# Gated delta layer, products P and A: two heads alternate on two row groups, exponentials ahead of the third copy, two unread products fewer

## The reference, cut to what matters

```python
def _step(S, xs):
    qt, kt, vt, gt, bt = xs
    S = S * jnp.exp(gt)[..., None, None]
    pred = jnp.einsum('bhk,bhkv->bhv', kt, S)
    delta = (vt - pred) * bt[..., None]
    S = S + jnp.einsum('bhk,bhv->bhkv', kt, delta)
    return (S, jnp.einsum('bhk,bhkv->bhv', qt, S))
```

## Time and profile before

| what | us |
|---|---|
| median of 3 runs | 1492.69 (1489.96 to 1498.32) |
| the profiled execution, its own time | 1490.81 |
| its span | 1489.1 |
| granted clock of TensorE, mean over the span | 0.939 of full |
| PE, DVE, ACT, POOL busy | 1355.1, 895.7, 695.8, 277.0 |
| the block of the change, from the first transposition to the end of the last L1509 | 396.6 to 429.3 |

### The profile page before, as it was taken

The page is one execution under the profiler, slowest core; times in us unless marked ns, Lnnn a source line. Parts: engine busy times, 40 slices in busy tenths (PEclk is TensorE's granted clock), DMA queues, the critical chain, the costliest instruction groups (busy, mean ns, idle before and its releaser), DMA issues. The chain is left out here.

```text
span 1489.1 us, 32883 instructions
## 1 busy us (share of the span) xinstructions
PE 1355.1 (91%) x13699; PEld 748.7 (50%) x13707; DVE 895.7 (60%) x2139; ACT 695.8 (47%) x1038; POOL 277.0 (19%) x343
## 2 busy tenths in 40 slices
PE   7999997998578987989999989988699999989989
PEld 3355554464346773644555454445245555564436
DVE  3899984646685456649999555323455555525331
ACT  5578786635373226536777732102344444442110
POOL 4331431002320000043000001101433433200210
PEclk9999998999788998999999989999599999989999
DMA  3323301000300000032221030002100000000000
GB/s 88 65 35 69 67 3 33 1 2 0 114 1 4 16 1 15 1 61 34 37 43 24 3 103 0 0 9 48 20 12 16 15 13 15 7 1 1 1 0 28
DMA packets 33958, 37.48 MB, mean 25 GB/s; under 512 B 9153, under 2 KB 24626, under 8 KB 33810
## 3 DMA queue, kind: packets, MB, share of 16 engines
q1 hardware_dynamic: 33810, 35.39, 10.9%
HBM read 18.43 MB, written 1.07 MB: 13 GB/s over the span
## 5 line engine op out<-in xcount | busy, mean ns | idle before, releaser
L586 DVE TENSOR_REDUCE row_max_pieces<-psum 128x1 f32<-128x512 f32 (+3 forms) x672 | 407.1, 647 | 123.1 <-PE psum L481 121.0
L685 ACT ACTIVATE probs<-psum 128x1024 f32<-128x1024 f32 (+7 forms) x384 | 343.5, 899 | 218.2 <-PE psum L481 217.8
L535 PE MATMUL psum<-probs,v_ones 128*32 128x256 f32 (+1 forms) x2688 | 239.2, 377 | 8.5 <-POOL probs L470 4.1
L481 PE MATMUL psum<-q_all,k_head 97*32 97x512 f32 (+3 forms) x1536 | 192.3, 492 | 3.5 <-issue 3.5
L481 PE MATMUL psum<-k_stack,q_stack 96*32 96x512 bf16 x2048 | 162.6, 387 | 5.4 <-DVE row_max_pieces L586 3.1
L481 PE MATMUL psum<-q_stack,k_stack 97*32 97x512 bf16 x2048 | 160.7, 385 | 0.0
L535 PEld LDWEIGHTS psum<-probs,v_ones 128*32 128x32 f32 x2688 | 88.2, 109 | 85.5 <-POOL probs L470 21.1
L481 PE MATMUL psum<-k_head_bf,q_all_bf 80*32 80x512 bf16 (+3 forms) x768 | 96.2, 347 | 5.0 <-POOL q_all_bf L2500 3.6
L481 PEld LDWEIGHTS psum<-q_all,k_head 97*32 97x32 f32 x1536 | 78.8, 110 | 34.4 <-issue 8.6
L481 PEld LDWEIGHTS psum<-k_stack,q_stack 96*32 96x32 bf16 x2048 | 57.9, 97 | 72.2 <-DVE row_max_pieces L586 20.4
L481 PEld LDWEIGHTS psum<-q_stack,k_stack 97*32 97x32 bf16 x2048 | 59.1, 97 | 51.1 <-ACT probs L685 3.7
(11 more groups left out here) (363 smaller groups left out, 2085.3 us busy)
## 6 DMA issues: line engine op xcount, KB each, us to landing
q_stack<-arena SPq DMA_DIRECT2D x32, 96.0 KB, 2.6
k_stack<-arena SPq DMA_DIRECT2D x32, 96.0 KB, 2.6
arena<-gd_g_sums SPq DMA_DIRECT2D x6, 512.0 KB, 6.1
q_stack<-arena SPq DMA_DIRECT2D x32, 64.0 KB, 2.3
k_stack<-arena SPq DMA_DIRECT2D x32, 64.0 KB, 2.3
x_tokens<-in_x SPq DMA_DIRECT2D x4, 256.0 KB, 3.2
k_stack<-arena SPq DMA_DIRECT2D x32, 32.0 KB, 2.3
q_stack<-arena SPq DMA_DIRECT2D x32, 32.0 KB, 2.0
```

Of the source, the lines that this page charges most:

```text
L481: last = pe.matmul(o[j:j + 32], by[:, j:j + 32], rows, **flags)
L535: last = pe.matmul(psum[32 * g:32 * g + VW, PVB, a - g * D:D], V[:, c, h, :], pr[:, n % PB, a:(g + 1) * D], start=(c == 0), stop=(c == (2 ...
L586: last = dve.reduce_max(mx[:, h % 2, qt, i:i + 1], o[:, 0:plain], AX.X)
L685: act.activation(pr[:, n % PB, q_from(c):], psum[:, 2 * (n % 2):2 * (n % 2) + 2, :].rearrange("p a n -> p (a n)")[:, q_from(c):], ACT.Exp, ...
```

## The change

- `p_and_a(n)` now does pieces n and n+1 together, for even n: for each j it multiplies the chunk of head h, then that of head h+1, on the neighbouring 32 rows and into the other slot.
- The wait for `a_done` stands once for the pair and is for n-1: pieces up to n-2 have been read.
- The turns stand after j = 0 and j = 1 (in the first pair after j = 0, 1 and 2), two for a pair.
- `keep_busy` is gone from the head of pieces 0, 2 and 4; one stands behind the first pair. With the one ahead of the third `turn`, two remain of four.
- ACT: `decays(0)` stands ahead of keep(2).

```diff
-                TURNS_IN = ((3, 4), (5,)) + tuple((m,) for m in range(6, len(turns)))
+                TURNS_IN = ((3, 4, 5),) + tuple((m, m + 1) for m in range(6, len(turns), 2))
...
-                            h, half = blocks[n]
-                            f, rows = h // 4, slice(32 * (h % 4), 32 * (h % 4) + 32)
+                            (h, half), f = blocks[n], blocks[n][0] // 4
                             for odd in range(2):
                                 pe.wait_ge(kept[odd], (EACH * (2 * f + half + 1) + 1 - odd) // 2)
-                            if n >= 3:
-                                pe.wait_ge(a_done, n - 2)
-                            if n in (0, 2, 4):
-                                keep_busy(pe, 2 + 2 * (n % 3), 1)
+                            if n >= 2:
+                                pe.wait_ge(a_done, n - 1)
                             for j in range(4):
                                 cols = slice((4 * half + j) * P, (4 * half + j + 1) * P)
-                                last = pe.matmul(slot(n)[:, j // 2, j % 2], KNT[rows, f, cols], QKT[rows, :, f, cols],
-                                                 start=True, stop=True)
-                                if j == 3:
-                                    last.then_inc(pa_in, 1)
-                                if j % 2 and j // 2 < len(TURNS_IN[n]):
-                                    turn(TURNS_IN[n][j // 2])
+                                for i in range(2):
+                                    rows = slice(32 * ((h + i) % 4), 32 * ((h + i) % 4) + 32)
+                                    last = pe.matmul(slot(n + i)[:, j // 2, j % 2], KNT[rows, f, cols], QKT[rows, :, f, cols],
+                                                     start=True, stop=True)
+                                    if j == 3:
+                                        last.then_inc(pa_in, 1)
+                                if j < len(TURNS_IN[n // 2]):
+                                    turn(TURNS_IN[n // 2][j])
...
-                        for n in range(len(blocks)):
+                        for n in range(0, len(blocks), 2):
                             p_and_a(n)
+                            if n == 0:
+                                keep_busy(pe, 6, 1)
...
                         keep(0)
+                        decays(0)
                         keep(2)
-                        decays(0)
                         decays(1)
```

## The result

| | before | after |
|---|---|---|
| median of the runs (4 each), us | 1492.87 (1489.96 to 1498.32) | 1508.51 (1507.98 to 1515.4) |
| ratio | | 1.012, 95% interval 1.0099 to 1.014 |
| span of the profiled execution, us | 1489.1 | 1506.2 |
| mean granted clock | 0.939 | 0.930 |

A forecast was written before the change was run, and what follows sets the result against it. PE, which does not rest, was taken to bound the block, with DVE last at its end. Waits less savings 4.3 plus clock fall 10.4 gave 14.7 us: 1505.5 on the profiled execution, 1507.4 on the median; said 1506, range 1494 to 1513.

The forecast's parts named there:

- The head: Block start through first pair: first product 0.95 us earlier, second pair at 406.3 against piece 2 at 407.74, gaining 1.4 us.
- The price of 0.20 + 0.43k: PE's time in us for k products on each of two row groups side by side: 0.63, 1.06, 1.49.
- The wait: Ahead of later pairs PE waits 1.64 us for DVE's reading; pairs 5.08 against 3.26 us, block +4.3 at held clock.
- The rival of the wait that does not bite: PE runs ahead into the next pair, its queue stays full; block ends 3.0 us earlier, 1487.8; chance 0.06.
- the rival of serial products: Alternating products do not overlap, 1.72 us more per pair; +14.6, again about 1506; chance 0.07.
- The clock: In the changed block the granted clock falls near 412 to 414 and does not come back: +10.4 us.
- three and a half pairs: Number of pairs taken to run at half clock, 2.96 us more each: +10.4; bounds one and a half and five.
- The pair at half clock: Products, turns and wait of one pair after the clock falls: 8.04 us, 2.96 more than at full clock.
- The rival of the held clock: The clock holds and the wait stays: +4.3 us, 1495.1 to 1497.0; chance 0.27.
- the two unread products: Products nobody reads, dropped from PE's work in the block: 1.06 us saved each, included in the +4.3.
- the x8 row: PE timeline row before the change: four products of two adjoining pieces take what two take alone, so overlap already exists.

The follow-up runs named there:

- e_last: Changed kernel with the two turns of each pair, from the second pair on, moved behind the pair's last products, into the wait: 1494.34 us, ratio 1.0009.
- e_busy: Changed kernel with one unread product of 512 columns in each of the four waits ahead of pairs 4, 6, 8 and 10: 1496.11 us, ratio 1.0038.
- e_fewer: Kernel before the change, without the unread products at the heads of pieces 2 and 4: 1501.67 us, ratio 1.0061.
- e_mix: Changed kernel's head, then from piece 2 on the order and waits of before, without further unread products: 1502.89 us, ratio 1.0057, runs in two groups.
- e_wait: Kernel before the change, with the pair's stricter wait (a_done for n-1) at even pieces and the old product order: 1497.72 us, ratio 1.004.

## Why the prediction was right

*The head.* Forecast: first product at 399.75, first pair ending at 404.0, second pair at 406.3. Measured: 399.73, 404.01, 406.30. The price of 0.20 + 0.43k for k products on each of two row groups holds for k = 1 (399.73 to 400.36, 0.63) and for k = 4 (e_last).

*The wait.* Forecast 1.64 us ahead of each of the last four pairs; the rows show 1.66 to 1.67 of idleness. The forecast said that PE never stood in the block before; it did once, 0.69 us ahead of 399.64, which changes none of its sums. With the clock held the forecast was 4.3 us, and e_busy shows 4.2. The rival of the wait that does not bite falls: nothing passed it. So does the rival of serial products.

*The clock.* It fell, as forecast. I had it fall near 412 to 414, so that three and a half pairs pay; it was 0.50 from about 410.9, and four pairs paid: 4 x 2.96 + 4.3 = 16.1, which is what the block lost. That half pair is most of what the forecast lacks. The pair at half clock was forecast at 8.04 and is 8.04. The rival of the held clock had 0.27 and falls for this kernel; e_busy is that case made, at 1496.1 inside its 1495 to 1497.

What bore the forecast of the clock was one stretch of before, and I misread it: I took the 1.93 us of idleness for what came ahead of the fall. By the rows, PE was still at work when the clock stood at 0.50, and the idleness began only at 472.54 (474.47 less 1.93):

```profile
472.20:472.40 0.20, 0.12 (x2) 0.13 (x1) 0.14 (x1) 0.00 (x0) 0.00 (x0) 0.97 0.00 0
472.40:472.50 0.10, 0.10 (x1) 0.00 (x0) 0.10 (x1) 0.00 (x0) 0.00 (x0) 0.50 0.00 0
```

What stood ahead of that fall was narrow work, 3.23 us busy of 3.40. e_fewer then lost the clock without any idleness. So the fall in the changed kernel was forecast rightly on a reason that was half wrong, and in that part the hit is luck. What the runs leave is this: e_busy, with more full-row work in the waits, and e_last, with the same work in shorter pairs, held the clock; e_fewer, without idleness but with one head at a time up to the fall, lost it. No run separates idleness, the rows in use and the unread products from each other.

The Trainium skill, in "TensorE: Matmul & The Clock Gate", section "Why this matters for your kernels", names idle gaps between bursts of matmuls as what drops the clock. e_fewer has none in the 6.80 us ahead of its fall, and the measurement decides.

The Trainium skill, in "TensorE: Matmul & The Clock Gate", section "Part 3: Packing small matmuls", has products on distinct row groups run concurrently. The trace agrees: 0.63 us for one of each head.

*What I did not see.* I counted the two unread products as a saving of 1.06 us each. In the changed kernel they may be that or not; in the kernel before, taking both out cost 10 us of block length, and taking out one saved 2.1.

*Open.* Whether an execution of e_mix holds the clock changes between runs of the same kernel. I take it that small shifts in time decide; only one of its runs has a trace. The head alone does not settle it: e_mix, the changed kernel and e_busy have the same head, and from the first transposition on the clock fell after about 10.9 us in e_mix, after 14.2 in the changed kernel, and not at all in e_busy's block. Why the inversion had a lower clock after the change than before (0.60 against 0.78) was not tried.

## What to carry to other kernels

Before taking out "useless" matmuls, read the granted clock over the stretches around them: at 32 rows a product the engine can be busy all the time and still lose half its clock, as in e_fewer. When two pieces of work are made to finish together, their consumer starts later by one piece: count the buffers again, for three slots that decouple single pieces do not decouple pairs. And look whether the overlap that an edit is to bring is there already; the x8 row showed that it was.

## What the runs showed of the hardware

- TensorE's granted clock fell from 1.00 to 0.50 (2.4 to 1.2 GHz) while PE was busy for 6.80 of 6.80 us, and stayed there over 29.90 busy us (e_fewer). The work was products on 32 rows by 128 columns, one head's at a time up to the fall, and float32 transpositions. At 1.00, with two heads side by side, the same kinds of work held for 13.4 us (414.10 to 427.50, before).
- Four products that stand in the queue as two of one row group and then two of the other take 1.07 us (413.42 to 414.49, e_wait), as two of one head do. A wait between the two groups that lasts until the first group is through takes the overlap away, though it shows as next to no idleness: 2.19 us (415.05 to 417.24, e_wait).
- Eight float32 products of 256 columns, alternating over two row groups and two banks, take 1.92 us (e_last). At the rate of full rows, 0.43 us each, eight would take 3.44.
